# Recurrent weights split during the attention, input products beside recurrence tile 0, and the FFN in 22 chunks

## What is computed

```python
x = x + _L0_attn_ref(_L0_cond_ref(x, cond_2048, Wq, Wk, Wv, b), Wq, Wk, Wv, Wo)
x = x + _L0_ffn_ref(_L0_cond2_ref(cond_2048, x, W_ih, W_hh, b_ih, b_hh), gate_w, gate_b, bias, w1, b1, w2, b2)

# _L0_cond2_ref: D = 512, one step for each position, h of 8 x 512
gi = x @ W_ih + b_ih
gh = h @ W_hh + b_hh
r = jax.nn.sigmoid(i_r + h_r)
z = jax.nn.sigmoid(i_z + h_z)
n = jnp.tanh(i_n + r * h_n)
h_new = (1.0 - z) * n + z * h

# _L0_ffn_ref: E, TOP_K, D, H = 8, 2, 512, 352
scores = xf @ gate_w.T + gate_b + bias
top_scores, top_idx = jax.lax.top_k(scores, TOP_K)
gates = jax.nn.softmax(top_scores, axis=-1)
comb = jnp.sum(jax.nn.one_hot(top_idx, E, dtype=gates.dtype) * gates[..., None], axis=1)
h = jax.nn.silu(jnp.einsum('td,ehd->teh', xf, w1) + b1)
y = jnp.einsum('teh,edh->ted', h, w2) + b2
out = jnp.einsum('ted,te->td', y, comb)
```

## Time and profile before

| | us |
|---|---|
| median of 3 runs (2253.45 to 2257.80) | 2255.41 |
| the profiled execution, by its own time | 2256.26 |
| its span in the profile | 2254.4 |
| second attention, up to | 713.7 |
| idle of TensorE until W_ih has landed, up to | 725.2 |
| input products and splits, up to | 911.3 |
| recurrence tile 0, up to | 1069.9 |
| tiles 1 to 7, up to | 2165.6 |
| the tail | 88.8 |

### The profile page before, as it was taken

The page is one execution under the profiler, slowest core; times in us unless marked ns, Lnnn a source line. Parts: engine busy times, 40 slices in busy tenths (PEclk is TensorE's granted clock), DMA queues, the critical chain, the costliest instruction groups (busy, mean ns, idle before and its releaser), DMA issues.

```text
span 2254.4 us, 81286 instructions
## 1 busy us (share of the span) xinstructions
PE 2034.8 (90%) x34730; PEld 1736.8 (77%) x34730; DVE 1500.9 (67%) x5717; ACT 796.8 (35%) x2842; POOL 228.5 (10%) x346
## 2 busy tenths in 40 slices
PE   5899999999977989655999999999999999999999
PEld 3677777767756868555798888888888888888877
DVE  3475576566654089566777777777777777777753
ACT  1365364455533222222333332333333333333332
POOL 0011011101102100000001010110110110101012
PEclk9999999999988999655999999999999999999999
DMA  6000000000001922100000000000000000000000
GB/s 247 1 1 1 1 1 1 1 1 1 1 1 65 313 72 73 51 17 3 17 17 17 13 17 18 26 3 18 27 3 27 17 17 13 17 17 13 3 11 10
DMA packets 53643, 66.36 MB, mean 29 GB/s; under 512 B 4385, under 2 KB 45793, under 8 KB 52417
## 3 DMA queue, kind: packets, MB, share of 16 engines
q1 hardware_dynamic: 50832, 46.48, 6.2%
q0 software_dynamic: 2448, 14.68, 1.9%
HBM read 44.34 MB, written 16.81 MB: 27 GB/s over the span
## 4 chain that ended last, share of the span: by engine, by line
PE 45%; DVE 12%; issue 2%; DVEq 0%; DMA 0%; POOL 0%; ACT 0%; ACTq 0%
PE ps L1291 24%; PE ps L1243 9%; PE ps L1223 9%; DVE hn L1403 2%; DVE s L1403 2%; PE ps L1276 2%; DVE hp L1439 2%; DVE dh L1435 1%; DVE hp L1442 1%; DVE hn L1419 1%; DVE hn L1421 1%; PE ps L1232 1%; DVE dh L1429 1%; DVE ns L1431 1%; DVE h L1440 0%
## 5 line engine op out<-in xcount | busy, mean ns | idle before, releaser
L1291 PE MATMUL ps<-hp,whf 128*128 128x32 f16 x24576 | 661.4, 178 | 105.5 <-DVE hp L1442 101.1
L1291 PEld LDWEIGHTS ps<-hp,whf 128*128 128x128 f16 x24576 | 645.0, 97 | 143.8 <-DVE hp L1442 136.3
L1223 PE MATMUL ps<-cur,w1f 128*128 128x256 f16 x2304 | 296.0, 276 | 0.0
L1243 PE MATMUL ps<-hh,w2f 128*128 128x256 f16 x2304 | 290.4, 274 | 0.0
L1322 ACT ACTIVATE rz<-s 128x32 f32<-128x32 f32 x512 | 117.3, 229 | 472.4 <-DVE s L1403 472.4
L1385 POOL TENSOR_TENSOR hh<-tb,hh 128x256 f16<-128x256 f32 x192 | 130.1, 682 | 1331.5 <-ACT hh L1360 1331.5
L1223 PEld LDWEIGHTS ps<-cur,w1f 128*128 128x128 f16 x2304 | 225.6, 99 | 34.0 <-issue 6.1
L1243 PEld LDWEIGHTS ps<-hh,w2f 128*128 128x128 f16 x2304 | 210.3, 98 | 43.6 <-issue 19.9
L1403 DVE SCALAR_TENSOR_TENSOR s<-ps,sc,gi 128x32 f32<-128x32 f32 x512 | 126.0, 246 | 172.5 <-PE ps L1291 159.9
L946 PE MATMUL ps<-x1T,wi 128*128 128x256 f32 x768 | 171.7, 385 | 20.1 <-DMA wi<-in_W_ih 12.1
L946 PEld LDWEIGHTS ps<-x1T,wi 128*128 128x128 f32 x768 | 147.4, 193 | 44.0 <-DMA wi<-in_W_ih 12.5
(11 more groups left out here) (195 smaller groups left out, 2903.3 us busy)
## 6 DMA issues: line engine op xcount, KB each, us to landing
gi_d<-stage SPq DMA_DIRECT2D x96, 128.0 KB, 1.7
gi<-gi_d SPq DMA_DIRECT2D x16, 768.0 KB, 5.2
w1f<-in_w1T POOLq DMA_DIRECT2D x4, 1408.0 KB, 9.5
xall<-in_x SPq DMA_DIRECT2D x4, 1024.0 KB, 9.2
x1T<-in_xT SPq DMA_DIRECT2D x1, 4096.0 KB, 21.8
w2f<-in_w2T POOLq DMA_DIRECT2D x2, 2048.0 KB, 11.6
out<-x1T SPq DMA_DIRECT2D x8, 512.0 KB, 2.9
wi<-in_W_ih SPq DMA_DIRECT2D x1, 3072.0 KB, 10.3
```

The lines of the kernel that those rows point to most:

```text
L1223: last = nc.tensor.matmul(ps[:, 6 + i % 2, 0:TT], w[:, wp, e % EH, c * P:(c + 1) * P], cur[:, k, hq, :, :].rearrange("p s b -> p (s b)"), ...
L1243: last = nc.tensor.matmul(ps[:, 4 + m // 2, (m % 2) * TT:(m % 2 + 1) * TT], w[:, wp, e % EH, m * P:(m + 1) * P], hh[:, i % RING, hq, :], s ...
L1291: last = nc.tensor.matmul(ps[:, bank, g * WIDE * 2 * B:(g + 1) * WIDE * 2 * B], whp[:, k, w, q, g * P:(g + 1) * P], wide(hp[:, k, :, :].re ...
```

## The change

It has four parts. (1) W_hh is loaded at the start of the first attention, in a new object `Recurrent` that lives over all blocks. Its maximum and scale factors are taken by VectorE before the first rotation of the second attention; GpSimd splits it there in 48 pieces of 128 columns, eight after each batch's masks. The attention's weights lie in the room of W_ih, which is loaded by SP after the last v product. The copy `hb` goes.

(2) `prepare` is replaced by `first_tile`. It forms the 12 input units of tile 0 straight into `gi`, then runs the 32 steps of tile 0 with the other 84 units between them (two or three a step), the maxima of w1 and w2 in steps 1 to 16, their scales in steps 17 to 20, and their splits in steps 20 to 31: ScalarE scales a piece, VectorE casts it, GpSimd subtracts. w1, w2 and the small tensors are loaded by SP.

(3) In the recurrence, gi and the biases carry the scale of the products, so that VectorE adds with plain tensor_tensor and ScalarE's functions undo the scale. `nxt` and `cur` give way to `hs`, two buffers of a tile.

(4) The FFN's 8 x 352 hidden rows are cut into 22 full chunks, so some chunks hold rows of two experts. The gates are split into fp16 halves, transposed (TensorE), and broadcast by one fp16 matmul with a selection matrix for each of 14 expert pairings; `cb` has six buffers. The selection matrices are made by VectorE after the first step of tile 1.

```diff
-NCH = NE * FC
+NCH = NE * HF // P
...
-        while load[s] >= 3 + (s % MORE == 1) or at[-2:] == [s, s]:
+        while load[s] >= 3 or at[-2:] == [s, s]:
...
+                    if name == "attn_WkT":
+                        sp.dma_start(gru.whf[:, :, :, :, :].rearrange("p k q a n -> p k (q a n)"),
+                                     ins["W_hh"].rearrange("(k p) n -> p k n", p=P)).then_inc(gru.d_whh, 16)
...
+                for b in range(B):
                     diagonals(b)
+                    if b == 0:
+                        pool.wait_ge(v_sc, 1)
+                    for j in range(8 * b, min(8 * b + 8, len(at))):
+                        split(j)
...
+                sp.wait_ge(p_v, B + 1)
+                sp.dma_start(gru.wi[:, :, :], ins["W_ih"].rearrange("(k p) n -> p k n", p=P)).then_inc(gru.d_wi, 16)
...
-                pe.wait_ge(d_w, 64)
-                pe.wait_ge(d_tab, 16)
-                pe.wait_ge(v_init, 3)
+                pe.wait_ge(d_qk, 32)
...
+                recurrent_maxima()
+                recurrent_scales()
                 rotate(0)
...
+                for s in range(SPT):
+                    t.pe_step(s)
+                    if s == MAXIMA_DONE + 1:
+                        pe.wait_ge(v_a, S_BASE)
+                        for i in range(4):
+                            last = nc.tensor.transpose(ps[0:1, 7, i * P:(i + 1) * P], mxa[:, i:i + 1], ident)
+                        last.then_inc(p_a, 1)
+                    if s == SCALES_AT:
+                        pe.wait_ge(v_a, S_BASE + 1)
+                        nc.tensor.matmul(ps[:, 7, 0:4], ones1, mx1[:, :], start=True, stop=True)\
+                            .then_inc(p_a, 1)
+                    for u in range(NQ, UNITS):
+                        if UNITS_AT[u - NQ] == s:
+                            unit(u)
...
+                    if u - NQ >= 4:
+                        act.wait_ge(d_st[u % 4], 16 * ((u - NQ) // 4))
...
+                    evict(due_now[0])
+                    for j in range(NPIECES):
+                        if SPLIT_AT[j] == s:
+                            src, _, width, scale = piece(j)
+                            if j == 0:
+                                act.wait_ge(v_sc, 1)
+                            if j >= 2:
+                                act.wait_ge(g_w, j - 1)
+                            nc.scalar.activation(tmp[:, j % 2, 0:width], src, ACT.Copy,
+                                                 scale=sc[:, scale:scale + 1]).then_inc(a_w, 1)
+                    for u in due_now[1:]:
+                        evict(u)
...
+                for j in range(NPIECES):
+                    _, half, width, _ = piece(j)
+                    pool.wait_ge(v_w, j + 1)
+                    nc.gpsimd.tensor_tensor(half[:, width:2 * width], tmp[:, j % 2, 0:width], half[:, 0:width],
+                                            ALU.subtract).then_inc(g_w, 1)
...
+                            dve.wait_ge(a_w, j + 1)
+                            nc.vector.tensor_copy(half[:, 0:width], tmp[:, j % 2, 0:width]).then_inc(v_w, 1)
...
-                    add_scaled(hn[:, :, :], of_bank(1)[:, :, 1, :], hn[:, :, :], v_ab)
+        tt(hn[:, :, :], part(1, 1), hn[:, :, :], ALU.add).then_inc(self.v_hn, 1)
...
-                        nc.tensor.matmul(ps[:, 3, 0:TT], ident[0:NE, e:e + 1].broadcast_to((NE, P)),
-                                         combT[:, :], start=True, stop=True).then_inc(p_bc, 1)
+                        nc.tensor.matmul(ps[:, 3, 0:TT], selm[:, n, :], gates[:, :], start=True, stop=True)\
+                            .then_inc(p_bc, 1)
```

More of the change, by code:

```diff
@@ L778, with segments @@
 K_STEPS = 2 + 2 * (HEAVY // 8) + 5 * (HEAVY % 8)
-NCH = NE * FC
+def segments(c):
+    found, j = [], c * P
+    while j < (c + 1) * P:
+        e = j // HF
+        end = min((e + 1) * HF, (c + 1) * P)
+        found.append((e, j - e * HF, j - c * P, end - c * P))
+        j = end
+    return found
+GATES_OF = [tuple((e, p0, p1) if len(segments(c)) > 1 else (e, 0, P) for e, _, p0, p1 in segments(c))
+            for c in range(NCH)]
+SELECTIONS = sorted(set(GATES_OF), key=GATES_OF.index)
+SEL_OF = [SELECTIONS.index(g) for g in GATES_OF]
+NSEL = len(SELECTIONS)
 DOWN_FIRST, DOWN_LAST = 10, 38
@@ new lines, in store @@
+                def store(u):
+                    tile, q = u // NQ, u % NQ
+                    sp.wait_ge(a_i, u - NQ + 1)
+                    sp.dma_start(t.gi_d[:, q, tile * SPT:(tile + 1) * SPT, :].rearrange("p s b -> p (s b)"),
+                                 stage[:, u % 4, :]).then_inc(d_st[u % 4], 16)
+                for u in range(NQ, UNITS):
+                    if u - NQ == (UNITS - NQ) * 5 // 8:
+                        sp.wait_ge(t.v_h, (SPT // 2) * 4)
+                        for j in range(4):
+                            sp.wait_ge(d_st[j], 16 * NQ // 4)
+                        t.load(sp, 1, 0)
+                    store(u)
@@ L1044, in pow2, with maxima @@
+                def maxima(j):
+                    if j < 8:
+                        dve.wait_ge(d_w1, 16 * KD)
+                        step(big(mx[:, 0, j:j + 1], w1flat[:, j, :]))
+                    else:
+                        dve.wait_ge(d_w2, 16 * sum(len(segments(c)) for c in range(NCH)))
+                        step(big(mx[:, 1, j - 8:j - 7], w2flat[:, (j - 8) * W2P:(j - 7) * W2P]))
                 def pow2(i, j):
@@ L1298, in step @@
-                def step(n):
-                    ready(pe, v_h, n * 4)
-                    products(0, 0).then_inc(p_r, 1)
-                    products(1, 2).then_inc(p_n, 1)
-                    products(2, 1).then_inc(p_z, 1)
-                def tile(t, recur, now, late, steps=SPT):
-                    for s in range(steps):
-                        if recur:
-                            step(t * SPT + s)
-                        ffn_slice(t - 1, s, now, late)
-                start(pe, p_r, p_n, p_z, p_sc, p_ct, p_bc, p_up, p_dn)
@@ L1362, in tile @@
-                def tile(t, recur, now, late, steps=SPT):
-                    for s in range(steps):
-                        if recur:
-                            step(t * SPT + s)
-                        ffn_slice(t - 1, s, now, late)
-                        if recur:
-                            keep(t * SPT + s, t, s)
-                act.preload_act_table_set("sigmoid_and_others")
-                start(act, a_r, a_z, a_t, a_ar, a_g, a_cb, a_sg, a_h)
-                tile(0, True, False, False)
@@ L1373, in _ @@
[L1373 to L1377 removed]
+                                             bias=b1[:, i:i + 1], scale=sc[:, S_UN1:S_UN1 + 1]).then_inc(a_sg, 1)
+                    for i, g in due(CAST_AT, s, f, now, late):
+                        j = g * NCH + i
+                        ready(act, v_u, j + 1)
+                        ready(act, p_dn, j - RING + 1)
+                        nc.scalar.activation(hh[:, j % RING, 0, :], tb[:, j % TB, :], ACT.Copy).then_inc(a_h, 1)
@@ L1379, in _ @@
             @block.gpsimd
             def _(pool):
-                def tile(t, now, late, steps=SPT):
-                    for s in range(steps):
-                        for i, g in due(REST_AT, s, t - 1, now, late):
-                            ready(pool, a_h, g * NCH + i + 1)
-                            nc.gpsimd.tensor_tensor(hh[:, i % RING, 1, :], tb[:, i % TB, :], hh[:, i % RING, 0, :],
-                                                    ALU.subtract).then_inc(g_l, 1)
-                start(pool, g_l)
```

924 lines of the change are left out of this document (515 added, 409 removed).

## The result

The changed kernel takes 2167.29 us (median of 4 runs, 2165.18 to 2170.91) against 2255.02 before: a ratio of 0.9616 (95% interval 0.9604 to 0.9629), 88 us less. 2102 was forecast, with a range of 2064 to 2150: the sign was right and the size wrong by 65 us. The profiled execution has 2168.39 us and a span of 2166.6.

What follows compares the result with a forecast made beforehand. For 356 us two successive stages filled neither TensorE nor VectorE; the rest was near TensorE's length. Terms +4 - 86.7 - 2 - 59 - 9.7 = -153.4 from 2256.3, less 0.9, gave 2102 us; range 2064 to 2150.

Steps and rivals of the forecast that it cites:

- Attention, +4 (0 to +10): First attention to 713.7: net +0.9 from the recurrent weights' maxima and +3 from GpSimd's split pieces meeting VectorE's normalisations.
- Preparation and tile 0, -86.7: From 713.7 to step 32: 269.5 us instead of 356.2, input units beside tile 0's steps; bounds -107 and -62.
- the rival Clock: Beside tile 0, TensorE would run at the lower of its two clock levels: total 2267, slower; chance 0.02.
- the splits: Tile 0, steps 20 to 31: 19 weight pieces, GpSimd's subtractions holding VectorE, 18 us; ends 0 and 36.
- the stall: Early tile 0: ScalarE waits for a staging buffer behind SP's 64 loads, 3 us; ends 0 and 15.
- The rival Locked: Tile 0: splits cost twice as much and loads stall ScalarE 10 us more, total 2127; chance 0.15.
- Tile 1, -2: Tile 1 gains as the others, but building selection matrices on VectorE costs some 7 us; -6 to +2.
- Tiles 2 to 7, -59: Six steady tiles: 147 us each instead of 156.9, TensorE bounding most steps; -35 or -73 at the ends.
- steps 7 to 10 have doubled gate operations (2): Steady tiles: one of the waits that stay, 2 us of 7 in a tile, from doubled gate operations.
- the rival Chain: Steady tiles' gate chain: fused and plain operations cost the same when reading PSUM, total 2126; chance 0.13.
- tiles at 151 us or more: Tiles 2 to 7: the sign given for the gate chain bounding, where 147 us a tile was forecast.
- Tail, -9.7: Tail, 88.8 us before: fewer groups -5.9, broadcasts 5.0 to 1.7, cur copy -2, longer wait for the choice +1.5.

Runs made afterwards that it cites:

- experiment 5: Changed kernel with both halves of an up chunk in one slice, plus ScalarE's three step operations scaling by an instruction constant, not an SBUF value (results differ): 2115.79 us.

## Why the prediction was wrong, step by step

**Attention, +4 (0 to +10): too high, about 0.** TensorE's first unit started at 714.0, where 718.3 was forecast. GpSimd is busy 151.7 instead of 85.0 us there, yet the stage from 47 on lasts 666.0 us and lasted 666.7 before, with TensorE busy 609 and 612. The half microsecond a batch for held operations did not show. This was read from the traces alone; no run separates the locks from the earlier start.

**Preparation and tile 0, -86.7: in sign and place right, 17.5 short.** The units beside the steps were as costed: steps of 7.67 and 5.94 us against 7.6 and 5.9, and no lower clock (the rival Clock is refuted: 1.00 in the first units, 0.95 in tile 0). The first 12 units took 20.8 us (20.7 forecast), and the change of blocks about what was forecast. Short were: the splits, 29 instead of 18, since steps 20 and 21 alone last 14.8 and 13.6 us: there the small operations, counted at 2 us, stand behind the held second casts and are held themselves (17 us went by spreading); the stall, 7.3 instead of 3; and 0.08 us in each of 31 steps, 2.5 in all. The rival Locked had the mechanism and a price of 25 in all; it was 15. Its own terms, the splits twice (+18) and the loads 10 longer, add up to 28. The upper bound of the stage, -62, is too low too: with the ends that the prediction gives, 36 for the splits and 15 for the stall, it is -56.7.

**Tile 1, -2: wrong, +8.** 9.8 instead of 7 us for what its first step adds, the 6 us of steps 7 to 10 of the next point, and 1.4 of the operand.

**Tiles 2 to 7, -59: this is the step that failed, -14 measured.** The prediction's "steps 7 to 10 have doubled gate operations (2)" looked at these steps, and saw VectorE's work but not what waits for it. I had costed each step by PE's groups or by the chain, whichever is longer, as if neither queue had a wait of its own in it. The ups' wait for the product two chunks back is in the code before and after; that it had never been late before was due to the pairing, which the new chunk count broke. The table of halves alone would have told: a distance of one slice had become none. It cost 5.9 us a tile, 35 in tiles 2 to 7, part of it by the lower clock; with the halves paired, tiles 2 to 7 are 36.3 of the 44.6 us shorter. 8.3 are left. A second term was left out there: ScalarE's operand puts 92 ns on the chain where PE waits for it, 1.4 us a tile by experiment 5, an estimate of 8.4 in six tiles. Most tiles of experiment 5, without the operand, take 145.9 to 146.4 us where 147 was forecast, so other terms were put somewhat too high, and a few steps stretched at the lower clock made up for it (one in tile 4 of the kernel with the halves paired takes 5.9 us instead of 4.4, at a granted clock of 0.59). I did not separate these further. The chain's other half was right: additions of PSUM products (L1090) take 190 ns, 200 assumed, so the rival Chain is refuted by its own row. Its sign, tiles at 151 us or more, did show (154.3), for another reason: a time for a tile doesn't name the wait in it.

**Tail, -9.7: -12.1,** right within 2.4.

The sum of the bounds, "2058 and 2158", doesn't come out of the terms: with -56.7 for the second one and all bounds one way it is 2060 and 2166. The range given, up to 2150, had no room for a wait that the sum didn't contain.

## What to carry to other kernels

When a change renumbers a table of slots, recompute for every double-buffered resource the distance in slots from its release to its next claim, and compare it with the old one; a distance of zero puts one engine's whole step into another's queue, and an assertion that allows equality hides it. Cost a step by each queue in order, with its waits in it, not by the sum of its work. Before an operation goes to GpSimd for relief, compare its length there with the gap until VectorE's next two-input operation; where it didn't fit into the gap, here, VectorE was quicker alone.

## What was unexpected in the hardware

- A short idle can be paid twice: after PE's waits of 2.22 and 1.60 us in slices 7 and 8 of one tile the granted clock was 0.50 from 1516 to 1522 us, and the step took 8.3 us. In the tile where it was 1.00 again behind such waits, the step took 5.9.
- A scale read from SBUF costs ScalarE some 92 ns an operation of 128x32 (321 against 229, the shortest of each).
- A subtraction of 1408 columns takes 2.86 us on GpSimd and 1.63 on VectorE; 1024 columns, 2.13 and 1.23.
- The stall of the stores had two causes of the same length. With 28 of 64 issues taken off SP's queue, a store of 128 KB took up to 13.2 us to land for 1.7 at best.
